# Graph convolution: one product for three turns of the vectors, one for three vector components, operands copied dense by ScalarE

## Chip, core and metric

One NeuronCore of a Trainium2 chip runs the whole program. The metric is the device time of one execution in microseconds, taken as the median of the runs shown. Engines are named as in the profile: PE (TensorE), DVE (VectorE), ACT (ScalarE), POOL (GpSimd), SP (SyncE).

## What is computed

A graph network of four layers on 12,500 nodes and 400,000 edges, each layer added to x and normalised. The change concerns the last layer, an equivariant convolution over edges. A node's 32 features are 8 scalars and 8 vectors of three components. Each edge has a weight (from which a small network makes 384 radial numbers) and a unit direction r. Cut to what matters:

```python
R = relu(abs_distances[:, None] @ w1 + b1) @ w2 + b2      # 384 numbers an edge
Y = spherical_harmonics(rel_vec)                          # of the direction
Fj = features[src]
for i, (mo, lo) in enumerate(RS):                         # out: 8 scalars, 8 vectors
    for j, (mi, li) in enumerate(RS):                     # in: 8 scalars, 8 vectors
        for k, lf in enumerate(range(abs(lo - li), lo + li + 1)):
            acc += _NORM[i] * einsum('euv,ef,evi,ofi->euo', Rb[..., k], Yf, Fb, C)
out = zeros.at[dst].add(msg)
```

The kernel writes this with v·r (how far a vector points along the direction), v x r (the crossed vector), v itself and the scalars: 256 radial numbers weigh 16 factors (8 scalars, 8 times v·r) and 128 weigh, for each component, 16 numbers (8 of v, 8 of v x r).

## The kernel before

Edges come sorted by destination in groups of 512: 128 partitions by `PER` = 4 columns j. The convolution (`convolve`) works through 832 groups, in 208 turns of a loop that has `SLOTS` = 4 groups written out; `s` is the group's place in the turn, `c = s % 2` chooses one of two buffers. `turns` writes the first and the last turn apart.

`after_hops` normalises x and makes the table of rows to be gathered: `CONV` = 88 floats a node, 8 scalars and then five blocks of 16 floats (`BLOCK`), of which the first 8 hold vector component 0, 1, 2, 0, 1 and the other 8 are zero. It is stored to `conv_dram`.

In `convolve` each engine has its own program and they meet in semaphores.

- SP loads a group's edges (`rows`, 8 floats each: source, place, weight, direction, and the first direction components again) when `rows_free` is 2 (one from ACT, one from DVE) and then its weights.
- POOL gathers the 512 source rows (`far`) by four indirect DMAs when `far_free` is 2. Between the second and the third it does `fold_products` for a group two back: it waits for `products_made` and adds the halves of `products_a`.
- ACT makes `hidden` for the group after (L2098), copies the scalars of `far` into `factors` (L2114), makes `minus_local` (L2117), `away` (L2127) and `hot` (L2135), the matrix that sends edges to nodes.
- PE makes the radial numbers of the next group (L2156, L2157) when `radial_free` allows and `hidden` is ready, and then sums the messages of the group before into `part` (L2168).
- DVE does the rest, in `one_group`. For group s: three products of vectors with shifted directions, `turned` (L2220, 96 elements each). For the group before, p: `finish_b` (L2206, sums `products_b` over 16, 1536 elements read) and `finish_a` (L2198, 512 read, waits for the fold). For s: `factors` (L2258, v·r) and the cross product (L2261), written into the zeros of `far`. For p: `along_r` (L2227). For s: `products_a` (L2270, 1024). For p: `add_own` (L2232), which lets PE sum. For s: three products, `product_b` (L2275, 512 each, one per component), between them two calls of `accumulate` (L2239, 32 elements each) which add the node sums of group s - 2 to `sums`.

`step` gives each DVE instruction a count on one semaphore and `wait(n)` waits for that count. The queue is in order: whatever stands behind a wait is issued after it. The end of the group is this:

```python
product_b(2).then_inc(radial_free[c], 1)
if added:
    wait(n_added)
    dve.sem_inc(part_free[c], 1)
```

At the end of a turn there follow `wait()`, the loop's branch and `steps.restart()`, which clears the count.

Of the kernel before, what the change touches and what calls it, by code (L numbers as in the profile page):

```python
# [24 lines left out]
P = 128  # L25
# [38 lines left out]
CONV = MUL + 5 * BLOCK  # L64
# [1850 lines left out]
def after_hops(nc, k):  # L1915
# [67 lines left out]
def convolve(nc, k):  # L1983

    with stage(nc, k) as ctx:
# [20 lines left out]
        sum_b = sb("sum_b", [P, 3, PER, MUL], 2)  # L2006
# [8 lines left out]
        factors_ready, factors_free = sem("factors_ready", 2), sem("factors_free", 2)  # L2015
# [66 lines left out]
        def _(act):  # L2082
            for c in range(2):
# [4 lines left out]
                act.sem_inc(factors_free[c], 1)  # L2088
# [16 lines left out]
            def one_turn(i, first, last):  # L2105
                for s in range(SLOTS):
# [6 lines left out]
                    act.wait_ge(factors_free[c], turn(i, s, 2))  # L2113
                    act.copy(factors[c][:, :, 0:MUL], far[s][:, :, 0:MUL]).then_inc(copied, 1)  # L2114
# [8 lines left out]
                    act.wait_ge(copied, 1 + HALVES)  # L2123
# [10 lines left out]
                    act.wait_ge(copied, 1 + HALVES + PER)  # L2134
# [50 lines left out]
        def _(dve):  # L2185
# [16 lines left out]
            def finish_b(i, s):  # L2202

                dve.wait_ge(radial_free[s % 2], turn(i, s, 2) + 1)
                dve.sem_inc(far_free[s % SLOTS], 1)
                return step(dve.tensor_reduce(sum_b[s % 2][:].rearrange("p o j u -> p (o j u)"),  # L2206
                                              products_b[:].rearrange("p o j u m -> p (o j u) m"),
                                              AX.X, ALU.add))

            def direction(s, at):  # L2210

                return spread(rows[s % SLOTS][:, :, 3 + at:6 + at], 3, MUL)

            def blocks(s, at):

                return far[s][:, :, MUL + at * BLOCK:MUL + (at + 3) * BLOCK].rearrange("p j (o m) -> p j o m", m=BLOCK)

            def turn_vectors(s, n, at_v, at_r):

# [219 lines left out]
```

## Time and profile before

| | us |
|---|---|
| median of three runs | 29652.48 |
| lowest, highest | 29636.92, 29660.63 |
| the profiled execution | 29833.74 |
| its span, first to last instruction | 29831.7 |

The profiled execution is 0.6% above the median. The page gives busy time by engine, then the span in 40 slices; the convolution is the last seven or eight of them, where DVE stands at 9 tenths. A group of instructions is shown by line, engine, operation, the names written and read, how many there were, busy time, mean duration and the idle time before them. The timeline gives a start and a duration for each. Instructions of one engine are pipelined, so that a start can lie before the end of the one in front; instructions that only handle semaphores, registers and branches are not shown and appear as idle time if nothing runs beneath them. A matmul's end is modelled.

### The profile page before, as it was taken

The page shows a single profiled execution, that of the slowest core. Times are in us where ns is not written, and L with a number is a line of the kernel's source. Part 1 is how long each engine was busy: PE and PEld are TensorE (multiplying, and loading weights), DVE is VectorE, ACT ScalarE, POOL GpSimd, SP SyncE. Part 2 cuts the span into 40 slices and gives each one's busy share as a digit, 9 for nine tenths or more (in the row PEclk, how much of TensorE's full clock was granted, in tenths as well). Part 3 has the DMA queues.
Part 4 walks back from the last instruction along what each step waited for, and adds up shares of the span by engine and source line. Part 5 has one row for each costly group of instructions (what it writes and reads, how often), then busy time and mean ns, then how long its engine had stood idle before and what let it go on. Part 6 is the DMA issues. An engine that isn't in the chain of part 4 may idle for free. (4 is left out here: it accounts for less than half of the span.)

```text
span 29831.7 us, 294521 instructions
## 1 busy us (share of the span) xinstructions
PE 13941.6 (47%) x65171; PEld 13225.7 (44%) x65172; DVE 11715.7 (39%) x26884; ACT 5681.8 (19%) x18021; POOL 17107.9 (57%) x17490
## 2 busy tenths in 40 slices
PE   1333333333333357777433333333333358888887
PEld 1233323333333357777433333333333347777777
DVE  1376511111111145555211111111111159999999
ACT  6411222100000011111000000000000025555554
POOL 2677766366666620000366666666666667777777
PEclk8555555555555577777555555555555568888888
DMA  1111111322222210000000000200000032222223
GB/s 44 15 15 14 15 14 15 24 58 58 59 58 59 59 32 20 19 20 20 13 11 12 11 12 11 11 13 11 11 12 11 11 33 50 50 50 50 50 50 47
DMA packets 1840283, 855.51 MB, mean 29 GB/s; under 512 B 1295920, under 2 KB 1624849, under 8 KB 1839380
## 3 DMA queue, kind: packets, MB, share of 16 engines
q0 software_dynamic: 532480, 382.75, 9.8%
q1 hardware_dynamic: 1307008, 471.30, 7.1%
q14 instruction: 86, 0.70, 0.0%
q10 hardware_dynamic: 692, 0.49, 0.0%
q8 instruction: 17, 0.28, 0.0%
HBM read 757.65 MB, written 96.92 MB: 29 GB/s over the span
## 5 line engine op out<-in xcount | busy, mean ns | idle before, releaser
L937 POOL DMA_INDIRECT hop_far<-hop_rows,hop_index x6656 | 6280.0, 944 | 7187.6 <-issue 6005.5
L973 PE MATMUL hop_total<-hop_far,hop_hot 128*128 128x32 f32 x13312 | 3127.2, 376 | 6433.4 <-issue 3640.6
L973 PEld LDWEIGHTS hop_total<-hop_far,hop_hot 128*128 128x128 f32 x13312 | 3080.7, 322 | 6481.2 <-issue 6479.8
L743 POOL DMA_INDIRECT weighted_far<-in_x_dram,weighted_rows x3328 | 3410.8, 1025 | 2052.5 <-issue 1475.5
L952 DVE TENSOR_TENSOR hop_hot<-hop_iota,local_of_edge 128x512 f32<-128x512 f32 x1664 | 1092.8, 688 | 8405.0 <-DMA rows_by_src<-push_row,push_index 7087.8
L1048 POOL DMA_INDIRECT rows_by_src<-push_row,push_index x3328 | 3186.4, 957 | 1741.3 <-issue 1520.7
L2048 POOL DMA_INDIRECT conv_far<-conv_rows x3328 | 3174.6, 954 | 1050.5 <-issue 810.1
L2156 PE MATMUL conv_radial_a<-radial,conv_hidden 128*128 128x256 f32 x6656 | 2893.2, 523 | 792.3 <-DVE conv_products_b L2275 562.9
L1097 PE MATMUL push_near<-far_rows_sb,push_turned 128*128 x6656 | 1689.4, 436 | 3218.2 <-DVE push_turned L1075 1750.3
L826 PE MATMUL weighted_total<-weighted_message,weighted_hot 128*128 128x33 f32 x6656 | 1569.7, 399 | 3450.7 <-issue 1621.5
L1097 PEld LDWEIGHTS push_near<-far_rows_sb,push_turned 128*128 128x128 f32 x6656 | 1601.5, 327 | 3306.1 <-issue 3304.6
L826 PEld LDWEIGHTS weighted_total<-weighted_message,weighted_hot 128*128 128x128 f32 x6656 | 1486.5, 327 | 3534.7 <-issue 3534.3
L2156 PEld LDWEIGHTS conv_radial_a<-radial,conv_hidden 128*128 128x128 f32 x6656 | 1856.6, 327 | 858.4 <-issue 856.8
L2157 PEld LDWEIGHTS conv_radial_b<-radial,conv_hidden 128*128 128x128 f32 x6656 | 1992.7, 332 | 171.6
L924 ACT COPY hop_index<-source_of_edge 128x4 int32 (+1 forms) x1664 | 291.8, 193 | 9310.2 <-DMA rows_by_src<-push_row,push_index 7431.5
L2157 PE MATMUL conv_radial_b<-radial,conv_hidden 128*128 128x128 f32 x6656 | 1855.3, 367 | 0.0
L2275 DVE TENSOR_TENSOR conv_products_b<-conv_radial_b,conv_far 128x512 f32<-128x512 f32 x2496 | 1694.7, 679 | 0.0
L1071 DVE TENSOR_TENSOR push_place<-push_place,push_trash 128x4 f32<-128x4 f32 x832 | 137.7, 166 | 3939.5 <-DMA push_place<-place_by_dst 3437.7
L2206 DVE TENSOR_REDUCE conv_sum_b<-conv_products_b 128x96 f32<-128x1536 f32 x832 | 1449.3, 1742 | 0.2 <-DVE conv_products_b L2275 0.2
L849 ACT ACTIVATE weighted_message<-weighted_far,weighted_rows 128x32 f32<-128x32 f32 x3328 | 828.6, 311 | 2513.0 <-DMA weighted_far<-in_x_dram,weighted_rows 1819.1
L2068 POOL TENSOR_TENSOR conv_folded_a<-conv_products_a 128x512 f32<-128x512 f32 x832 | 1053.8, 1267 | 350.3 <-issue 232.8
L1770 PE MATMUL att_part<-att_b_message,att_b_hot 128*128 128x132 f32 x7040 | 1247.3, 335 | 4.3 <-DVE att_b_message L1675 4.3
(250 smaller groups left out, 20408.4 us busy)
## 6 DMA issues: line engine op xcount, KB each, us to landing
push_line<-local_by_group SPq DMA_DIRECT2D x832, 256.0 KB
hop_far<-hop_rows,hop_index POOLq DMA_INDIRECT x6656
conv_weights<-weight_by_group SPq DMA_DIRECT2D x832, 128.0 KB
att_far<-rows_by_src SPq DMA_DIRECT2D x880, 80.0 KB
weighted_far<-in_x_dram,weighted_rows POOLq DMA_INDIRECT x3328
rows_by_src<-push_row,push_index POOLq DMA_INDIRECT x3328
conv_far<-conv_rows POOLq DMA_INDIRECT x3328
weighted_rows<-edges_by_dst SPq DMA_DIRECT2D x1664, 8.0 KB
```

The costliest lines, as they stand in the source:

```text
L743: pool.indirect_dma_start(far[s][:, j, :], None, table, bass.IndirectOffsetOnAxis(ap=rows[s][:, j, 0:1].bitcast(I32), axis=0)).then_inc(ga ...
L826: last = pe.matmul(total[:].rearrange("p n c -> p (n c)")[:, bass.ds(at[s * HALVES + j // COLUMNS], width)], hot[s][:, j, :], message[s][: ...
L937: pool.indirect_dma_start(far[s][:, j, :], None, table, bass.IndirectOffsetOnAxis(ap=index[s][:, j:j + 1], axis=0)).then_inc(gathered[s], 16)
L973: last = pe.matmul(total[:].rearrange("p n c -> p (n c)")[:, bass.ds(at[s * HALVES + j // COLUMNS] * F, F)], hot[s][:, j, :], far[s][:, j, ...
L1048: pool.indirect_dma_start(k.rows_by_src, bass.IndirectOffsetOnAxis(ap=index[s][:, j:j + 1], axis=0), row[s][:, j, :], None).then_inc(writt ...
L1097: last = pe.matmul(near[:, b, j * FAR:(j + 1) * FAR], turned[b][:, :, j], k.far_rows[:].rearrange("p b w -> p (b w)")[:, bass.ds(at[s * HA ...
L1770: last = pe.matmul(part[s % 2][:, 0:HEADS * W], b_hot[b][:, j, :], b_message[b][:, j, :], start=(j == 0), stop=(j == PER - 1))
L2048: pool.indirect_dma_start(far[s][:, j, :], None, k.conv_dram, bass.IndirectOffsetOnAxis(ap=rows[s][:, j, 0:1].bitcast(I32), axis=0)).then_ ...
L2156: pe.matmul(radial_a[:, c, j, :], hidden[c][:, :, j], k.radial[:, 0:256], start=True, stop=True)
L2157: last = pe.matmul(radial_b[:, c, j, :], hidden[c][:, :, j], k.radial[:, 256:384], start=True, stop=True)
L2206: return step(dve.tensor_reduce(sum_b[s % 2][:].rearrange("p o j u -> p (o j u)"), products_b[:].rearrange("p o j u m -> p (o j u) m"), AX ...
L2275: return dve.tensor_tensor(products_b[:, o], radial_b[:, c].rearrange("p j (u m) -> p j u m", m=BLOCK), spread(blocks(s, 0)[:, :, o, :], 2 ...
```

## The change

The gathered row becomes 64 floats: 8 scalars and seven components of 8 floats (0, 1, 2, 0, 1, 2, 0), without zeros. ACT copies, for each group, the three shifted directions of an edge into `around` (3 x 3), the vector components into the first halves of `pair` (3 components of 16) and, as before, the scalars into `factors`; it then releases a new semaphore `taken`. `rows_free` comes from ACT alone now, and `far_free` from DVE comes right behind `turned`. A semaphore `used` tells ACT that `around`, `pair` and `factors` of a slot may be written again. On DVE one product of 288 elements makes all of `turned`, one of 1536 makes all of `products_b`, whose order is by column and then component. The second `accumulate` stands behind it.

```diff
-CONV = MUL + 5 * BLOCK
+CONV = MUL + 7 * MUL
...
+def windows(tile, first, dims):
+
+    whole = tile[:]
+    return bass.AP(whole.tensor, whole.offset + first, [list(whole.ap[0])] + [list(d) for d in dims])
...
-            s.step(dve.memset(table[:], 0.0))
-            s.wait()
             s.step(dve.tensor_copy(table[:, :, 0:MUL], k.x[:, :, 0:MUL]))
-            for o in range(5):
-                at = MUL + o * BLOCK
+            for o in range(7):
+                at = MUL + o * MUL
                 s.step(dve.tensor_copy(table[:, :, at:at + MUL], vectors[:, :, o % 3, :]))
...
-        turned = [sb(f"turned_{n}", [P, PER, 3, MUL], 2) for n in range(3)]
-        factors = sb("factors", [P, PER, 2 * MUL], 2)
+        turned = sb("turned", [P, PER, 3, 3, MUL], 2)
+        factors = sb("factors", [P, PER, 2 * MUL], SLOTS)
+        pair = sb("pair", [P, PER, 3, BLOCK], SLOTS)
+        around = sb("around", [P, PER, 3, 3], SLOTS)
...
-        products_b = sb("products_b", [P, 3, PER, MUL, BLOCK], 1)[0]
+        products_b = sb("products_b", [P, PER, 3, MUL, BLOCK], 1)[0]
...
-                sp.sem_inc(rows_free[s], 2)
+                sp.sem_inc(rows_free[s], 1)
...
-                    sp.wait_ge(rows_free[s], 2)
+                    sp.wait_ge(rows_free[s], 1)
...
-                    act.wait_ge(factors_free[c], turn(i, s, 2))
-                    act.copy(factors[c][:, :, 0:MUL], far[s][:, :, 0:MUL]).then_inc(copied, 1)
+                    if not first:
+                        act.wait_ge(used[s], i)
+                    act.copy(around[s][:], windows(rows[s], 3, [(BY_DST, PER), (1, 3), (1, 3)])).then_inc(copied, 1)
+                    act.copy(pair[s][:, :, :, 0:MUL], far[s][:, :, MUL:4 * MUL].rearrange("p j (o m) -> p j o m", m=MUL)
+                             ).then_inc(copied, 1)
+                    act.copy(factors[s][:, :, 0:MUL], far[s][:, :, 0:MUL]).then_inc(copied, 1)
...
-                    act.wait_ge(copied, 1)
-                    act.sem_inc(factors_ready[c], 1)
+                    act.wait_ge(copied, 3)
+                    act.sem_inc(taken[s], 1)
                     act.sem_inc(far_free[s], 1)
...
-                dve.sem_inc(far_free[s % SLOTS], 1)
...
+            def turn_vectors(s):
+
+                return step(dve.tensor_tensor(
+                    turned[s % 2][:].rearrange("p j n o m -> p (j n o m)"),
+                    windows(far[s], MUL, [(CONV, PER), (2 * MUL, 3), (1, 3 * MUL)]),
+                    windows(around[s], 0, [(1, PER * 9), (0, MUL)]), ALU.mult))
...
-                n_along = turn_vectors(s, 0, 0, 0)
-                turn_vectors(s, 1, 2, 1)
-                n_turned = turn_vectors(s, 2, 1, 2)
+                dve.wait_ge(taken[s], i + 1)
+                n_turned = turn_vectors(s)
...
                 wait(n_turned)
-                n_crossed = step(dve.tensor_tensor(blocks(s, 0)[:, :, :, MUL:BLOCK], turned[1][c][:], turned[2][c][:],
+                dve.sem_inc(far_free[s], 1)
+                n_factors = step(dve.tensor_reduce(factors[s][:, :, MUL:2 * MUL],
+                                                   turned[c][:, :, 0].rearrange("p j o v -> p j v o"), AX.X, ALU.add))
+                n_crossed = step(dve.tensor_tensor(pair[s][:, :, :, MUL:BLOCK], turned[c][:, :, 1], turned[c][:, :, 2],
                                                    ALU.subtract))
...
-                    dve.sem_inc(rows_free[p % SLOTS], 1)
+                    dve.sem_inc(used[p % SLOTS], 1)
                     add_own(p)
-                wait(n_crossed)
-                step(product_b(0))
+                if added:
+                    n_added = accumulate(i, s - 2, 0, bins[0])
                 wait(n_products)
                 dve.sem_inc(products_made, 1)
-                dve.sem_inc(factors_free[c], 1)
+                wait(n_crossed)
+                dve.tensor_tensor(products_b[:].rearrange("p j o u m -> p (j o u m)"),
+                                  spread(radial_b[:, c], 2, 3),
+                                  spread(pair[s][:].rearrange("p j o m -> p (j o) m"), 2, MUL), ALU.mult
+                                  ).then_inc(radial_free[c], 1)
                 if added:
-                    n_added = accumulate(i, s - 2, 0, bins[0])
-                step(product_b(1))
-                if added:
-                    for h in range(1, HALVES):
-
-                        wait(n_added)
-                        n_added = accumulate(i, s - 2, h, bins[h])
-                product_b(2).then_inc(radial_free[c], 1)
-                if added:
+                    wait(n_added)
+                    n_added = accumulate(i, s - 2, 1, bins[1])
                     wait(n_added)
                     dve.sem_inc(part_free[c], 1)
```

## Rows read from the trace of the kernel before

**Rows 1.** The page: busy time of each engine over the whole span, times, share, instructions

```profile
PE 13941.6 (47%) x65171; PEld 13225.7 (44%) x65172; DVE 11715.7 (39%) x26884; ACT 5681.8 (19%) x18021; POOL 17107.9 (57%) x17490
```

**Rows 2.** Windows: busy us of each engine in this stretch of the convolution

```profile
25000.00:29500.00 4500.00, 3697.93 (x16369) 3445.37 (x16368) 4487.77 (x10231) 2329.57 (x6139) 3465.88 (x3411) 0.86 0.24 50
```

**Rows 3.** Timeline, DVE, one group: start, us, engine, line, op, out<-in, count

```profile
26902.76 0.58 DVE L2220 TENSOR_TENSOR conv_turned<-conv_far,conv_rows 128x96 f32<-128x96 f32 x3
26903.27 1.74 DVE L2206 TENSOR_REDUCE conv_sum_b<-conv_products_b 128x96 f32<-128x1536 f32 x1
26904.93 0.67 DVE L2198 TENSOR_REDUCE conv_message<-conv_folded_a 128x64 f32<-128x512 f32 x1
26905.52 0.25 DVE L2258 TENSOR_REDUCE conv_factors<-conv_turned 128x32 f32<-128x96 f32 x1
...
26905.86 0.25 DVE L2227 TENSOR_TENSOR conv_message<-conv_rows,conv_message 128x96 f32<-128x96 f32 x1
26906.03 1.21 DVE L2270 TENSOR_TENSOR conv_products_a<-conv_radial_a,conv_factors 128x1024 f32<-128x1024 f32 x1
26907.16 0.24 DVE L2232 TENSOR_TENSOR conv_message<-conv_message,conv_sum_b 128x96 f32<-128x96 f32 x1
26907.33 0.68 DVE L2275 TENSOR_TENSOR conv_products_b<-conv_radial_b,conv_far 128x512 f32<-128x512 f32 x1
26907.93 0.17 DVE L2239 TENSOR_TENSOR sums<-sums,conv_part 128x32 f32 x1
26908.02 0.68 DVE L2275 TENSOR_TENSOR conv_products_b<-conv_radial_b,conv_far 128x512 f32<-128x512 f32 x1
...
26908.72 0.68 DVE L2275 TENSOR_TENSOR conv_products_b<-conv_radial_b,conv_far 128x512 f32<-128x512 f32 x1
26909.32 0.58 DVE L2220 TENSOR_TENSOR conv_turned<-conv_far,conv_rows 128x96 f32<-128x96 f32 x3
```

**Rows 4.** Timeline, DVE: the last group of a turn, its start and its end

```profile
26915.88 0.58 DVE L2220 TENSOR_TENSOR conv_turned<-conv_far,conv_rows 128x96 f32<-128x96 f32 x3
...
26921.74 0.17 DVE L2239 TENSOR_TENSOR sums<-sums,conv_part 128x32 f32 x1
26921.83 0.68 DVE L2275 TENSOR_TENSOR conv_products_b<-conv_radial_b,conv_far 128x512 f32<-128x512 f32 x1
26922.58 0.60 DVE L2220 TENSOR_TENSOR conv_turned<-conv_far,conv_rows 128x96 f32<-128x96 f32 x3
```

**Rows 5.** The page, costliest groups: line, op, names, count, busy, mean ns, idle

```profile
L2206 DVE TENSOR_REDUCE conv_sum_b<-conv_products_b 128x96 f32<-128x1536 f32 x832 | 1449.3, 1742 | 0.2 <-DVE conv_products_b L2275 0.2
```

**Rows 6.** Timeline, DVE, after the last turn, where each step is waited for

```profile
29790.22 0.68 DVE L2198 TENSOR_REDUCE conv_message<-conv_folded_a 128x64 f32<-128x512 f32 x1
29790.93 0.26 DVE L2227 TENSOR_TENSOR conv_message<-conv_rows,conv_message 128x96 f32<-128x96 f32 x1
...
29791.92 0.53 DVE L2239 TENSOR_TENSOR sums<-sums,conv_part 128x32 f32 x2 [0.44 <-issue]
```

**Rows 7.** Timeline, ScalarE (ACT): first copy of the group that DVE takes up at 26922.58

```profile
26919.30 0.22 ACT L2114 COPY conv_factors<-conv_far 128x32 f32<-128x32 f32 x1
```

**Rows 8.** Timeline, GpSimd (POOL): fold running behind (first two) and in the middle

```profile
29745.00 1.27 POOL L2068 TENSOR_TENSOR conv_folded_a<-conv_products_a 128x512 f32<-128x512 f32 x1
...
29751.18 1.26 POOL L2068 TENSOR_TENSOR conv_folded_a<-conv_products_a 128x512 f32<-128x512 f32 x1
...
26907.47 1.26 POOL L2068 TENSOR_TENSOR conv_folded_a<-conv_products_a 128x512 f32<-128x512 f32 x1 [0.43 <-issue]
```

**Rows 9.** Timeline, DVE, near the stage's end: a group that starts on a late landing

```profile
29752.99 0.60 DVE L2220 TENSOR_TENSOR conv_turned<-conv_far,conv_rows 128x96 f32<-128x96 f32 x3 [0.19 <-DMA conv_far<-conv_rows]
```

**Rows 10.** Timeline between the hops and the convolution: table of rows and its store

```profile
24231.13 7.25 DVE L1931 MEMSET rows_of_conv<- 128x8624 f32 x1 [1.86 <-issue]
...
24238.89 3.00 DVE L1936 COPY rows_of_conv<-x 128x784 f32<-128x784 f32 x5
...
24242.39 16.45 SPq L1251 DMA_DIRECT2D conv_rows<-rows_of_conv  x1
```

More of the change, by code:

```diff
@@ L2014, in convolve @@
         radial_ready, radial_free = sem("radial_ready", 2), sem("radial_free", 2)
-        factors_ready, factors_free = sem("factors_ready", 2), sem("factors_free", 2)
+        taken, used = sem("taken", SLOTS), sem("used", SLOTS)
         hot_ready = sem("hot_ready", 2)
@@ L2204, in finish_b, with direction @@
                 dve.wait_ge(radial_free[s % 2], turn(i, s, 2) + 1)
-                dve.sem_inc(far_free[s % SLOTS], 1)
-                return step(dve.tensor_reduce(sum_b[s % 2][:].rearrange("p o j u -> p (o j u)"),
-                                              products_b[:].rearrange("p o j u m -> p (o j u) m"),
+                return step(dve.tensor_reduce(sum_b[s % 2][:].rearrange("p j o u -> p (j o u)"),
+                                              products_b[:].rearrange("p j o u m -> p (j o u) m"),
                                               AX.X, ALU.add))
[L2210 to L2218, printed above, removed]
-                return step(dve.tensor_tensor(turned[n][s % 2][:], blocks(s, at_v)[:, :, :, 0:MUL],
-                                              direction(s, at_r), ALU.mult))
+            def direction(s):
+                return spread(around[s % SLOTS][:, :, 0, :], 3, MUL)
+            def turn_vectors(s):
[3 more added lines that the diff above has]
+                    windows(around[s], 0, [(1, PER * 9), (0, MUL)]), ALU.mult))
             def vector_out(s):
@@ L2226, in along_r @@
             def along_r(s):
-                return step(dve.tensor_tensor(vector_out(s), direction(s, 0),
+                return step(dve.tensor_tensor(vector_out(s), direction(s),
                                               spread(message[s % 2][:, :, 4, :], 2, 3), ALU.mult))
             def add_own(s):
-                dve.tensor_tensor(vector_out(s), vector_out(s), sum_b[s % 2][:].rearrange("p o j u -> p j o u"),
+                dve.tensor_tensor(vector_out(s), vector_out(s), sum_b[s % 2][:],
                                   ALU.add).then_inc(message_ready[s % 2], 1)
@@ L2256, in one_group @@
                     n_a = finish_a(i, p)
-                wait(n_along)
-                n_factors = step(dve.tensor_reduce(factors[c][:, :, MUL:2 * MUL],
-                                                   turned[0][c][:].rearrange("p j o v -> p j v o"), AX.X, ALU.add))
                 wait(n_turned)
-                n_crossed = step(dve.tensor_tensor(blocks(s, 0)[:, :, :, MUL:BLOCK], turned[1][c][:], turned[2][c][:],
+                dve.sem_inc(far_free[s], 1)
+                n_factors = step(dve.tensor_reduce(factors[s][:, :, MUL:2 * MUL],
+                                                   turned[c][:, :, 0].rearrange("p j o v -> p j v o"), AX.X, ALU.add))
+                n_crossed = step(dve.tensor_tensor(pair[s][:, :, :, MUL:BLOCK], turned[c][:, :, 1], turned[c][:, :, 2],
                                                    ALU.subtract))
@@ L2265, in one_group @@
                     n_out = along_r(p)
-                dve.wait_ge(factors_ready[c], turn(i, s, 2))
                 dve.wait_ge(radial_ready[c], turn(i, s, 2))
@@ L2271, in one_group @@
                     products_a[:], radial_a[:, c].rearrange("p j (q m) -> p j q m", m=2 * MUL),
-                    spread(factors[c][:], 2, 2 * MUL), ALU.mult))
-                def product_b(o):
-                    return dve.tensor_tensor(
-                        products_b[:, o], radial_b[:, c].rearrange("p j (u m) -> p j u m", m=BLOCK),
-                        spread(blocks(s, 0)[:, :, o, :], 2, MUL), ALU.mult)
+                    spread(factors[s][:], 2, 2 * MUL), ALU.mult))
                 if before:
                     wait(max(n_out, n_sum))
-                    dve.sem_inc(rows_free[p % SLOTS], 1)
+                    dve.sem_inc(used[p % SLOTS], 1)
                     add_own(p)
-                wait(n_crossed)
-                step(product_b(0))
+                if added:
+                    n_added = accumulate(i, s - 2, 0, bins[0])
                 wait(n_products)
                 dve.sem_inc(products_made, 1)
-                dve.sem_inc(factors_free[c], 1)
-                if added:
-                    n_added = accumulate(i, s - 2, 0, bins[0])
-                step(product_b(1))
-                if added:
-                    for h in range(1, HALVES):
-                        wait(n_added)
-                        n_added = accumulate(i, s - 2, h, bins[h])
-                product_b(2).then_inc(radial_free[c], 1)
-                if added:
+                wait(n_crossed)
[3 more added lines that the diff above has]
+                                  ).then_inc(radial_free[c], 1)
+                if added:
+                    wait(n_added)
+                    n_added = accumulate(i, s - 2, 1, bins[1])
                     wait(n_added)
```

7 lines of the change are left out of this document (3 added, 4 removed).

## The prediction

> **What bounds the kernel now.** The profile's first two parts say that no engine is busy for the whole span [rows 1], so the question is the stage. The change touches only `after_hops` and `convolve`, and the convolution fills the last fifth of the span. The table of windows for 4500 us of it shows VectorE (DVE) busy 4487.77 us, 99.7%; TensorE is at 82% and GpSimd at 77% [rows 2]. So this stage's time is DVE's instruction stream, and what is to be counted is its time from one start to the next, not durations, since neighbours overlap.
>
> The DVE timeline of one group of 512 edges gives these steps [rows 3], from each start to the following one: three `turned` products 0.51 us together; `sum_b` 1.66; `finish_a` 0.59; `factors`, `crossed` (left out there, 26905.69) and `along_r` 0.17 each; `products_a` 1.13; `add_own` 0.17; `product_b(0)` 0.60; `accumulate` 0.09; `product_b(1)` 0.60; `accumulate` 0.10; `product_b(2)` 0.60. Sum 6.56 us (26902.76 to 26909.32). The group whose end is also the end of a loop turn takes 6.70 (26915.88 to 26922.58) [rows 4]. The page's `sum_b` row counts 832 groups [rows 5], so 208 turns of four: 3 x 6.56 + 6.70 = 26.38 us a turn.
>
> What a size costs: the steps of 0.095 (32 elements), 0.17 (96), 0.60 (512), 1.13 (1024) and 1.66 us (1536) lie on one line, 0.065 us plus 1.04 ns an element [rows 3]. Strided operands (`turned`, `along_r`), broadcast ones, PSUM ones and dense ones are all on it.
>
> **The change part by part.**
>
> *One `turned` product for three.* 288 elements once: 0.065 + 288 x 1.04 ns = 0.365 us for 0.51. Saves 0.145 a group.
>
> *One `products_b` for three.* 1536 elements are 1.66, the step of `sum_b` [rows 3], for 3 x 0.60 = 1.80. Saves 0.14. Its operands stay a broadcast PSUM array and a broadcast SBUF array, both kinds that are on the line already.
>
> *Where the second `accumulate` goes.* This is the part that decides. Before, it is issued under `product_b(2)`, which covers it: it costs 0.10 of the step, and the wait for its end before `part_free` is released is also covered, since `product_b(2)` runs on. After, it is the last instruction of the group, behind the whole `products_b`, and `wait(n_added)` stands between it and the next group's `turned`. Now its whole 0.17 us is on the path, then the sequencer's way out of that wait: release `part_free`, wait for `gathered`, wait for the new `taken`, issue. Nothing covers that. I call this gap G. The trace does not show it in the steady state. From below: `finish_a` ends at 29790.90 and `along_r`, which waits for it alone, starts at 29790.93: 0.03 us. From above: two accumulates in a row, each waited for, with register work and another wait between, take 0.53 for 2 x 0.17: 0.19 between them [rows 6], and 0.06 more if one wait more costs as much again: 0.25. I take 0.16, near the upper row, as it has the same sort of work in it. The group is then 0.365 + 1.66 + 0.59 + 3 x 0.17 + 1.13 + 0.17 + 0.10 + 1.66 + 0.17 + G = 6.36 + G = 6.52 us: of 0.285 saved by merging, only 0.04 is left.
>
> At the end of a turn the gap is longer, as the loop's branch, the clearing of the step counter and its registers come after that wait. That way is seen whole: the second accumulate ends at 26921.74 + 0.17 = 26921.91 and the next `turned` starts at 26922.58, 0.67 us later [rows 4]. Before, `product_b(2)` ran until 26922.51 beneath it and only about 0.15 was lost (6.70 against 6.56). After, all of it is open, with one more wait: 0.67 + 0.06 = 0.73 (up to 0.93, if the new wait's number has to be made in registers too). The group is 6.36 + 0.73 = 7.09 for 6.70.
>
> A turn: 3 x 6.52 + 7.09 = 26.65 for 26.38, +0.27 us, times 208 = **+56 us**. With G = 0.03 and 0.67 it is 3 x 6.39 + 7.03 = 26.20, -37 us; with 0.25 and 0.93, 3 x 6.61 + 7.29 = 27.12, +154 us.
>
> The Trainium skill speaks against both halves of this. Its page VectorE: DVE Perf Modes, section The DRAIN you can't avoid, says that the next operation does not start until the pipe is empty and that a semaphore between two operations costs nothing extra. By that the exposed wait would be free, and the sum would lie at the low end or under it. The same page's errata section gives an fp32 tensor-tensor instruction (N + 151) cycles at 0.96 GHz: 0.157 us fixed; four instructions fewer a group would then be 0.63 us, an estimate from that page, some 520 us in all. The rows show starts only 0.60 apart where a duration is 0.68 [rows 3]; so most of that fixed part is hidden already, and the trace disagrees for a stream that is never drained.
>
> *ScalarE's two more copies and the wait for them.* `pair` has 96 elements, `around` 36. The copy of 32 takes 0.22 us [rows 7]; none of the three is likely to pass 0.4, so `taken` comes at most 1.2 us after the copies begin at 26919.30. DVE takes up that group at 26922.58 [rows 4]: over 2 us are left. Cost 0 in the steady state. ScalarE itself is at 2329.57 of 4500 [rows 2], and adds under 0.7 of 6.56 us. Its wait for `used` asks for a group four back: 0. Behind it on ScalarE are `minus_local`, `away` and `hot`, for which TensorE waits a group later: covered. If the cover were gone, DVE would lose up to 0.7 us a group.
>
> *Gathers and loads.* Rows of 256 bytes for 352, the same four gathers. `far` and `rows` come free earlier (the first after `turned`, the second by ScalarE alone), so SP may load earlier. GpSimd is held by `fold_products`, which waits for `products_a`: not faster. Its own floor is seen where it runs behind, fold to fold 29745.00 to 29751.18 = 6.18 us, with no idle time listed before the fold; normally 0.43 is idle there [rows 8]. 6.18 is below 6.52, so it doesn't bind, and there was no 6.18 to gain either. `products_made` is released at the same place behind `products_a`.
>
> *`accumulate(0)`* goes ahead of `products_b`: its `part_ready` is two groups old. 0. TensorE sees `radial_free` about 0.25 us earlier after `add_own`. 0 for the end.
>
> *Last groups.* At the stage's end about a dozen groups have late gathers: the timeline has DVE waiting for the landing itself, as at 29752.99 [rows 9]. Now ScalarE's copies come in between, some 0.5 us each time: +6 us (0 to +13).
>
> *Between the stages.* The memset of 7.25 us goes, two more of the 0.60 us copies come, and the store, now 73% of the bytes behind a 16.45 us issue, may save 0 to 4.5, taken as 3 [rows 10]. -9 us (-6 to -11).
>
> **The sum.** 56 + 6 - 9 = +53 us. The profiled execution has 29833.74 us (span 29831.7), 0.6% above the median 29652.48; against its own time the forecast is 29887 us. Stage times are bound by fixed instruction times, so the same 53 us goes on the median: 29705 us. The bounds give -37 - 11 = -48 and 154 + 13 - 6 = +161: 29604 to 29813.
>
> **The rivals.**
> 1. *The wait at the group's end is nearly free* (G near 0.03, the loop's overhead not longer than now): 29604 to 29620 us. For it: the 0.03 row [rows 6]. Against: the 0.67 us at the turn is read directly and nothing is left to hide it.
> 2. *Each instruction removed brings more than its share of the pitch.* If the fixed part were all of 0.68 - 512 x 1.04 ns = 0.15 us, four fewer give 0.6 us a group for the 0.285 above, another 0.315 x 832 = 260 us: 29445 us. Against: five sizes on one line. That is the page's rule above, as far as rows can price it.
> 3. *Slower: DVE waits for `taken`.* ScalarE comes to its copies in order, after `hide`, which waits for the weights. Were the gathers' landing or the weights over 2 us later than now, each group would wait for ScalarE; at 0.5 us a group that is 416 us: 30120 us. Against: the 2 us of room.
>
> **How the numbers follow.** Forecast 0.74 (mechanism as told, -48 to +161), rival 1 0.10 (its end of that range or a little under), rival 2 or another gain 0.08, rival 3 0.08. A difference under 0.2%, 59 us, can't be told from none here. The forecast lies almost on that line: of its 0.74 I give 0.38 to slower and 0.36 to same. Same: 0.36 + 0.10 = 0.46; slower: 0.38 + 0.08 = 0.46; faster 0.08. The range 29604 to 29813 holds the forecast and rival 1, some 0.82; I keep 29600 to 29815.
>
> **What would show it.** In the profile after: `turned` at about 0.44 us and `products_b` at about 1.74 a piece, 832 each; in the DVE timeline a gap of 0.1 to 0.25 us before each `turned` and one of 0.7 to 0.9 at each turn, DVE's share in the windows falling to some 95%; a turn of 26.6 to 26.7 us. It is wrong if the gap is under 0.1 or a row leaves the line, if an idle time of DVE is put down to ScalarE, or if fold to fold nears 6.2.

## The result, and the profile after

The changed kernel takes 29737.51 us (median of 12 runs, 29698.96 to 29792.63), the kernel before in the same 12 rounds 29652.66: +85 us between the medians. The ratio is 1.0031, with a 95% interval of 1.0023 to 1.0039. It is slower, by a little more than the 59 us that the prediction took as the least that can be told from nothing. The forecast had been 29705, +53.

The profiled execution of the changed kernel has a span of 29716.6 us. That it is shorter than the span of the profiled execution before (29831.7) lies ahead of the part that was changed: the convolution's first `turned` starts at 24068.47 us there, at 24278.98 before. So the two are compared from that part on.

The page: busy time of each engine, then the two costliest groups of DVE (line, engine, operation, names, count, busy time, mean ns, idle before them).

```profile
PE 14044.8 (47%) x65171; PEld 13287.3 (45%) x65172; DVE 11532.7 (39%) x23557; ACT 5918.2 (20%) x19685; POOL 17144.8 (58%) x17490
...
L2287 DVE TENSOR_TENSOR conv_products_b<-conv_radial_b,conv_pair 128x1536 f32<-128x1536 f32 x832 | 1455.2, 1749 | 0.2 <-issue 0.2
L2214 DVE TENSOR_REDUCE conv_sum_b<-conv_products_b 128x96 f32<-128x1536 f32 x832 | 1452.2, 1745 | 0.2 <-DVE sums L2245 0.2
```

DVE has 3327 instructions fewer than in [rows 1], four a group, and is busy 183 us less. `products_b` is one instruction of 1749 ns beside `sum_b` of 1745 ns (1742 in [rows 5]): 1536 elements take the same time whether they are reduced or multiplied. DVE's work did become less. Now the windows for the same 4500 us as in [rows 2] (PE, PEld, DVE, ACT, POOL, granted clock, DMA share, GB/s):

```profile
25000.00:29500.00 4500.00, 3716.85 (x16055) 3427.27 (x16053) 4264.50 (x7357) 2482.23 (x7355) 3431.45 (x3344) 0.84 0.20 41
```

DVE was busy 4487.77 us of them and is now busy 4264.50, 94.8%. It waits 235 us and still bounds the stage. Where it waits is in its timeline (start, us, engine, line, operation, names, count, idle time before it); first the end of a turn and the group after it:

```profile
26761.56 0.17 DVE L2245 TENSOR_TENSOR sums<-sums,conv_part 128x32 f32 x1
26762.47 0.46 DVE L2224 TENSOR_TENSOR conv_turned<-conv_far,conv_around 128x288 f32<-128x288 f32 x1 [0.74 <-issue]
26762.85 1.75 DVE L2214 TENSOR_REDUCE conv_sum_b<-conv_products_b 128x96 f32<-128x1536 f32 x1
...
26766.74 0.25 DVE L2238 TENSOR_TENSOR conv_message<-conv_message,conv_sum_b 128x96 f32<-128x96 f32 x1
26766.91 0.18 DVE L2245 TENSOR_TENSOR sums<-sums,conv_part 128x32 f32 x1
26767.01 1.75 DVE L2287 TENSOR_TENSOR conv_products_b<-conv_radial_b,conv_pair 128x1536 f32<-128x1536 f32 x1
26768.67 0.17 DVE L2245 TENSOR_TENSOR sums<-sums,conv_part 128x32 f32 x1
26769.07 0.46 DVE L2224 TENSOR_TENSOR conv_turned<-conv_far,conv_around 128x288 f32<-128x288 f32 x1 [0.22 <-DVE sums L2245]
```

And the next end of a turn:

```profile
26782.26 0.46 DVE L2224 TENSOR_TENSOR conv_turned<-conv_far,conv_around 128x288 f32<-128x288 f32 x1 [0.22 <-DVE sums L2245]
...
26789.38 0.46 DVE L2224 TENSOR_TENSOR conv_turned<-conv_far,conv_around 128x288 f32<-128x288 f32 x1 [0.74 <-DVE sums L2245]
```

From one `turned` to the next a group inside a turn takes 6.60 us (26762.47 to 26769.07; 6.56 in [rows 3]) and one at a turn's end 7.12 (26782.26 to 26789.38; 6.70 in [rows 4]). Before `turned` stand idle times: 0.22 us in each group, where [rows 3] has none, and 0.74 at a turn, where [rows 4] has 0.07. Both stand behind the second `accumulate` (26768.67, 26761.56). The listing by lines, for 2000 us of this stage, adds them up:

```profile
L2224 DVE TENSOR_TENSOR conv_turned<-conv_far,conv_around 128x288 f32<-128x288 f32 x298 | 136.7, 459 | 105.3 <-DVE sums L2245 59.1 <-issue 46.3
```

105.3 us idle before 298 `turned`; that is all of DVE's idle time there.

Ahead of the stage, from the last step of the normalisation on (SPq is the store's issue):

```profile
24030.50 3.42 DVE L1221 TENSOR_TENSOR x<-norm_centred,norm_spread 128x3136 f32<-128x3136 f32 x1
...
24034.44 4.22 DVE L1940 COPY rows_of_conv<-x 128x784 f32<-128x784 f32 x7
...
24039.17 10.10 SPq L1257 DMA_DIRECT2D conv_rows<-rows_of_conv  x1
...
24068.47 0.46 DVE L2224 TENSOR_TENSOR conv_turned<-conv_far,conv_around 128x288 f32<-128x288 f32 x1 [10.41 <-ACTq L2130]
```

From that step to the first `turned` it is 37.97 us (24030.50 to 24068.47). Before it was 53.14 (24225.84 to 24278.98): the memset of 7.25 us and 1.86 idle in front of it are gone, the store's issue takes 10.10 for 16.45 us [rows 10], and two more copies have come. From the first `turned` to the update behind the convolution it is 5613.74 us (24068.47 to 29682.21) for 5518.32 (24278.98 to 29797.30): +95.4. With -15.2 that makes +80 of the 85 us; the other 5 are within the interval (68 to 116 us).

### The profile page after: what moved, and what is told of

Read it like the earlier page. It is cut to its first block and busy times, and to the rows that moved or that the text cites. A ratio compares the mean times of both kernels' runs of the same rounds, so it can differ in the third digit from the quotient of the medians.

```text
span 29716.6 us, 293058 instructions
## 1 busy us (share of the span) xinstructions
PE 14044.8 (47%) x65171; PEld 13287.3 (45%) x65172; DVE 11532.7 (39%) x23557; ACT 5918.2 (20%) x19685; POOL 17144.8 (58%) x17490
## 5 line engine op out<-in xcount | busy, mean ns | idle before, releaser
L2165 PE MATMUL conv_radial_a<-radial,conv_hidden 128*128 128x256 f32 x6656 | 2952.7, 533 | 635.1 <-DVE conv_products_b L2287 554.6
L2287 DVE TENSOR_TENSOR conv_products_b<-conv_radial_b,conv_pair 128x1536 f32<-128x1536 f32 x832 | 1455.2, 1749 | 0.2 <-issue 0.2
L2214 DVE TENSOR_REDUCE conv_sum_b<-conv_products_b 128x96 f32<-128x1536 f32 x832 | 1452.2, 1745 | 0.2 <-DVE sums L2245 0.2
```

The source lines that it names most:

```text
L2165: pe.matmul(radial_a[:, c, j, :], hidden[c][:, :, j], k.radial[:, 0:256], start=True, stop=True)
L2214: return step(dve.tensor_reduce(sum_b[s % 2][:].rearrange("p j o u -> p (j o u)"), products_b[:].rearrange("p j o u m -> p (j o u) m"), AX ...
L2287: dve.tensor_tensor(products_b[:].rearrange("p j o u m -> p (j o u m)"), spread(radial_b[:, c], 2, 3), spread(pair[s][:].rearrange("p j o ...
```

## The experiments

The kernels ran on more than one occasion, and the time of the kernel before was not the same in all (29652.66, 27341.17, 29625.73, 27372.80 us), because of stages ahead of the convolution: its first `turned` starts between 24019 and 24279 us in some traces and between 21776 and 21827 in the others. The convolution itself takes the same in both, within 5 us: the version with early accumulates takes 5258.5 us from the first `turned` to the update where its total is 27075.62 us, and 5263.8 (with one wait fewer) where it is 29366.42. Each kernel is therefore compared with the runs of the kernel before that were made beside it, and group lengths come from the traces.

The theory was that the time is lost where the group's last instruction is an `accumulate` that is waited for with nothing running over it; such a wait is called open below, and one under a running instruction covered. The rivals were the merged products themselves, ScalarE's copies with their new wait, and another engine close behind.

### Both accumulates early, in the changed kernel

```diff
                     n_out = along_r(p)
+                if added:
+                    n_added = accumulate(i, s - 2, 0, bins[0])
...
                     add_own(p)
                 if added:
-                    n_added = accumulate(i, s - 2, 0, bins[0])
+                    wait(n_added)
+                    n_added = accumulate(i, s - 2, 1, bins[1])
...
                 if added:
                     wait(n_added)
-                    n_added = accumulate(i, s - 2, 1, bins[1])
-                    wait(n_added)
                     dve.sem_inc(part_free[c], 1)
```

> The changed kernel, with the two accumulates moved ahead: the first behind along_r, the second behind add_own, so that products_b is the last VectorE instruction of a group and runs over everything the sequencer does at the group's and the turn's end. Theory (the changed kernel lost its time at the uncovered end of the group: 0.17 us of the last accumulate and a gap of 0.22, 0.74 at a turn): every group takes 6.60 - 0.17 - 0.22 + 0.10 = 6.30 us, also at a turn, so 208 x (26.91 - 25.20) = 356 us less than the changed kernel, about 29380 us, and faster than the kernel before by some 270. VectorE is then busy over 99% again. Rival A (the merged products or ScalarE's copies are what costs): the time stays within 50 us of the changed kernel. Rival B (another engine is just behind): GpSimd's fold to fold of 6.2 or TensorE's radial numbers take over, and the group stays at 6.4 or more, 29460 us or above.

Measured: 27075.62 us beside 27341.17, 0.990 (0.9885 to 0.9915), -266 us. DVE's timeline of one group:

```profile
24704.21 0.24 DVE L2233 TENSOR_TENSOR conv_message<-conv_around,conv_message 128x96 f32<-128x96 f32 x1
24704.38 0.17 DVE L2245 TENSOR_TENSOR sums<-sums,conv_part 128x32 f32 x1
...
24705.61 0.23 DVE L2238 TENSOR_TENSOR conv_message<-conv_message,conv_sum_b 128x96 f32<-128x96 f32 x1
24705.78 0.17 DVE L2245 TENSOR_TENSOR sums<-sums,conv_part 128x32 f32 x1
24705.88 1.74 DVE L2290 TENSOR_TENSOR conv_products_b<-conv_radial_b,conv_pair 128x1536 f32<-128x1536 f32 x1
24707.54 0.44 DVE L2224 TENSOR_TENSOR conv_turned<-conv_far,conv_around 128x288 f32<-128x288 f32 x1
```

Neither `accumulate` (24704.38, 24705.78) has idle time behind it, and `turned` starts 1.66 us after `products_b` (24705.88 to 24707.54), as [rows 3] have it for 1536 elements. A group takes 6.29 us, and there is no longer a difference at a turn. The windows of 2000 us:

```profile
24500.00:26500.00 2000.00, 1667.37 (x7632) 1567.68 (x7632) 2000.00 (x3500) 1181.23 (x3499) 1609.49 (x1591) 0.91 0.22 44
```

DVE is busy 2000.00 of 2000.00. The same merged products and the same copies are in this kernel, so they are not what costs (rival A). Rival B asked for 6.4 us or more. GpSimd is nearer than before, though not the bound; two folds of its timeline:

```profile
24712.21 1.27 POOL L2074 TENSOR_TENSOR conv_folded_a<-conv_products_a 128x512 f32<-128x512 f32 x1 [0.19 <-DVEq L2288]
...
24718.49 1.26 POOL L2074 TENSOR_TENSOR conv_folded_a<-conv_products_a 128x512 f32<-128x512 f32 x1 [0.17 <-DVEq L2288]
```

They are 6.28 us apart, at DVE's pace, and still 0.17 of it is idle before the fold.

### The same order of the last two instructions in the kernel before

```diff
                 step(product_b(1))
+                product_b(2).then_inc(radial_free[c], 1)
                 if added:
                     for h in range(1, HALVES):
 
                         wait(n_added)
                         n_added = accumulate(i, s - 2, h, bins[h])
-                product_b(2).then_inc(radial_free[c], 1)
                 if added:
                     wait(n_added)
```

> The kernel before with one edit: the second accumulate stands behind product_b(2) instead of in front of it; three turned products, three product_b and the wide rows stay. Theory: the same loss appears without the rest of the change. A group takes 6.56 - 0.10 + 0.17 + a gap of 0.15 (one wait fewer in it than in the changed kernel, no taken) = 6.78, and at a turn 6.63 + 0.67 = 7.30, so 3 x 6.78 + 7.30 = 27.64 us a turn for 26.39, +260 us: 29915 us. Rival A (the order of the last two instructions does not matter): within 30 us of the kernel before.

Measured: 27600.09 beside 27341.17 us, 1.0092 (1.0077 to 1.0107), +259 us. The first group here ends a turn:

```profile
25004.32 0.59 DVE L2220 TENSOR_TENSOR conv_turned<-conv_far,conv_rows 128x96 f32<-128x96 f32 x3
...
25010.79 0.17 DVE L2239 TENSOR_TENSOR sums<-sums,conv_part 128x32 f32 x1
25011.63 0.60 DVE L2220 TENSOR_TENSOR conv_turned<-conv_far,conv_rows 128x96 f32<-128x96 f32 x3 [0.68 <-DVE sums L2239]
...
25018.10 0.18 DVE L2239 TENSOR_TENSOR sums<-sums,conv_part 128x32 f32 x1
25018.43 0.60 DVE L2220 TENSOR_TENSOR conv_turned<-conv_far,conv_rows 128x96 f32<-128x96 f32 x3 [0.15 <-DVE sums L2239]
```

In this kernel with nothing else of the change the gap is there: 0.15 us behind the `accumulate` at 25018.10 and 0.68 behind that at 25010.79, which ends a turn. The latter group takes 7.31 us (25004.32 to 25011.63), the one after it 6.80. One pair of lines put the other way round costs 0.9% of the whole program. This shows the mechanism by itself. That expected and measured differ by 1 us is luck: the interval is some 40 us to either side, and the groups by themselves are 271 us longer (medians over the stage: 6.79 and 7.32 us, for 6.56 and 6.70), of which the last groups gave some back.

### One wait fewer in the gap

```diff
-                dve.wait_ge(gathered[s], (i + 1) * (16 * PER))
-
                 dve.wait_ge(taken[s], i + 1)
```

> The changed kernel without VectorE's own wait for gathered: taken is released by ScalarE only after its own wait for gathered, so the order is kept with one wait fewer in the gap before turned. Theory: what counts in the gap is how many things the sequencer handles one after another, so the gap falls from 0.22 to 0.15 and from 0.74 to 0.67, 832 x 0.07 = 58 us less than the changed kernel, about 29680 us. Rival: the gap is one fixed latency of draining the engine and the time stays, 29738 us.

Measured: 27368.31 beside 27341.17 us, 1.0011 (1.0002 to 1.0020), +27 us, where the changed kernel has +85: 58 less, as expected, though the interval leaves some 25 us to either side of the 27 alone. The traces are sharper: from the first `turned` to the update it is 5547.2 us for 5613.7.

```profile
25004.69 0.17 DVE L2245 TENSOR_TENSOR sums<-sums,conv_part 128x32 f32 x1
25005.51 0.46 DVE L2224 TENSOR_TENSOR conv_turned<-conv_far,conv_around 128x288 f32<-128x288 f32 x1 [0.65 <-DVE sums L2245]
...
25011.72 0.17 DVE L2245 TENSOR_TENSOR sums<-sums,conv_part 128x32 f32 x1
25012.04 0.46 DVE L2224 TENSOR_TENSOR conv_turned<-conv_far,conv_around 128x288 f32<-128x288 f32 x1
...
25018.56 0.46 DVE L2224 TENSOR_TENSOR conv_turned<-conv_far,conv_around 128x288 f32<-128x288 f32 x1
```

The gap is 0.15 us (25011.72 + 0.17 to 25012.04) for 0.22, and 0.65 for 0.74 at a turn; a group takes 6.52. So the gap is no fixed latency: one more satisfied wait in it costs 0.07 us, and 0.09 at a turn. The same edit was made where nothing is open:

> The version with both accumulates early, and without VectorE's own wait for gathered. In the changed kernel that wait cost 0.07 us a group; here it is handled under the running products_b. Theory: it costs nothing where it is covered, so a group stays at 6.29 us and the time within 10 us of the version with both accumulates early, 0.99 of the kernel before. Rival (a wait costs its 0.07 us wherever it stands): 6.22 us a group, 58 us less, 0.988.

Measured: 29366.42 beside 29625.73 us, 0.9912 (0.9896 to 0.9929). Its group is 6.29 us as without the edit. The rival's 0.988 lies outside the interval, and its group would be 6.22 us: a wait that is handled under a running instruction costs nothing here.

### Three products for one, accumulates between them

```diff
+                def product_b(o):
+                    return dve.tensor_tensor(
+                        products_b[:, :, o], radial_b[:, c].rearrange("p j (u m) -> p j u m", m=BLOCK),
+                        spread(pair[s][:, :, o, :], 2, MUL), ALU.mult)
...
```

with `product_b(0)`, `accumulate(0)`, `product_b(1)`, `accumulate(1)`, `product_b(2)` in the kernel before's order.

> The changed kernel with products_b as three products of 512 again (into the new layout, from pair) and the accumulates between them as before; ScalarE's copies, the single turned product and the narrow rows stay. Theory: a group is the one before less what the single turned product saves, 6.56 - 0.14 = 6.42, at a turn 6.42 + 0.2 = 6.62, so 25.88 us a turn for 26.39, 106 us less, and some 25 less outside the groups: 29520 us, 220 below the changed kernel although it has two instructions more a group. Rival A (ScalarE's copies or the wait for taken cost the time): it stays near 29740.

Measured: 27218.22 beside 27341.17 us, 0.9954 (0.9939 to 0.9970), -123 us, so some 208 below the changed kernel.

```profile
25000.55 0.44 DVE L2224 TENSOR_TENSOR conv_turned<-conv_far,conv_around 128x288 f32<-128x288 f32 x1
...
25006.36 0.67 DVE L2284 TENSOR_TENSOR conv_products_b<-conv_radial_b,conv_pair 128x512 f32<-128x512 f32 x1
25006.96 0.44 DVE L2224 TENSOR_TENSOR conv_turned<-conv_far,conv_around 128x288 f32<-128x288 f32 x1
...
25013.60 0.46 DVE L2224 TENSOR_TENSOR conv_turned<-conv_far,conv_around 128x288 f32<-128x288 f32 x1
```

A group takes 6.41 us and at a turn 6.64 (25006.96 to 25013.60). The version with two instructions more a group is faster, because the last of them covers the end. ScalarE's copies and `taken` are in it, and the group is as short as it was expected to be without a cost for them.

### Both accumulates behind

```diff
-                if added:
-                    n_added = accumulate(i, s - 2, 0, bins[0])
                 wait(n_products)
...
                 if added:
+                    n_added = accumulate(i, s - 2, 0, bins[0])
                     wait(n_added)
                     n_added = accumulate(i, s - 2, 1, bins[1])
```

> The changed kernel with the first accumulate moved behind products_b too, so that two waited steps stand open at the group's end. Theory: the first one loses its 0.10 of covered step and costs 0.17 plus a gap of 0.15 with register work in it, as in the tail of the kernel before: 6.60 + 0.23 = 6.82 us, 7.35 at a turn, 188 us above the changed kernel, 1.0095 of the kernel before. Rival (draining the engine once a group is the price, however many steps stand there): only the 0.07 of difference between covered and open length, 60 us above the changed kernel.

Measured: 29981.99 beside 29625.73 us, 1.0122 (1.0105 to 1.0139), +356. The changed kernel ran in the same rounds:

> The changed kernel itself, as the measure for the three beside it: 0.31% above the kernel before, some 85 us.

It took 29701.67, 1.0035 (1.0021 to 1.0049), +76. So the second open step costs 280 us and not 188, half as much again as expected; the groups account for some 258 of it (0.31 us in each).

```profile
25012.72 0.24 DVE L2238 TENSOR_TENSOR conv_message<-conv_message,conv_sum_b 128x96 f32<-128x96 f32 x1
25012.96 1.76 DVE L2285 TENSOR_TENSOR conv_products_b<-conv_radial_b,conv_pair 128x1536 f32<-128x1536 f32 x1
25014.63 0.50 DVE L2245 TENSOR_TENSOR sums<-sums,conv_part 128x32 f32 x2
25015.36 0.46 DVE L2224 TENSOR_TENSOR conv_turned<-conv_far,conv_around 128x288 f32<-128x288 f32 x1 [0.22 <-DVE sums L2245]
...
25022.26 0.46 DVE L2224 TENSOR_TENSOR conv_turned<-conv_far,conv_around 128x288 f32<-128x288 f32 x1 [0.22 <-DVE sums L2245]
```

A group takes 6.90 us (25015.36 to 25022.26), not 6.82. The two accumulates take 0.50 for 2 x 0.17, a gap of 0.16 as expected. The rest is at a place that had not been looked at: `products_b` starts 0.24 us after `add_own` (25012.72 to 25012.96), where 96 elements cost 0.17. `products_made` is released behind the end of `products_a`, and `products_b` is issued after that; in the changed kernel the first `accumulate` ran over just this wait (26766.74, 26766.91, 26767.01), unseen. That this 0.07 us is the uncovered issue is read from the trace; no run takes it away by itself. The rival, that draining the engine once is the whole price, is out: it asked for 60 us.

### How much room ScalarE has

```diff
+                    for n in range(8):
+                        act.copy(spare[:, n], far[s][:, :, MUL:4 * MUL]).then_inc(copied, 1)
                     act.copy(factors[s][:, :, 0:MUL], far[s][:, :, 0:MUL]).then_inc(copied, 1)
```

> The changed kernel with eight more copies of 96 elements on ScalarE in front of taken, written to a spare tile that nothing reads: about 8 x 0.17 = 1.4 us later for taken. Theory: in the changed kernel VectorE starts a group 3.65 us (median) after ScalarE's first copy of it, and the three copies and the release need 0.67, so 3 us are spare: a group stays at 6.60 and 7.12, and only the last twenty or so groups, whose gathers are late, lose about 1 us each: 0 to 20 us above the changed kernel. Rival (ScalarE's release is what VectorE waits for at the group's start): 1.4 x 832 = 1165 us more.

Measured: 29720.52 beside 29625.73 us, 1.0029 (1.0018 to 1.0041); the changed kernel had 1.0035 in the same rounds, its median 19 us lower. In the changed kernel ScalarE's first and last copy of a group are these, 0.51 us from the first start to the last end:

```profile
26765.13 0.22 ACT L2120 COPY conv_around<-conv_rows 128x36 f32<-128x36 f32 x1 [1.65 <-DMA conv_far<-conv_rows]
...
26765.43 0.21 ACT L2123 COPY conv_factors<-conv_far 128x32 f32<-128x32 f32 x1
```

With eight more in front of `taken`:

```profile
25000.21 0.22 ACT L2121 COPY conv_around<-conv_rows 128x36 f32<-128x36 f32 x1 [0.23 <-DMA conv_far<-conv_rows]
...
25000.51 1.47 ACT L2125 COPY conv_spare<-conv_far 128x96 f32<-128x96 f32 x8
25001.89 0.21 ACT L2126 COPY conv_factors<-conv_far 128x32 f32<-128x32 f32 x1
```

`turned` of that group comes at 25004.17, 3.96 us after the first copy, with the old 0.74 of a turn before it, and 0.22 in the group after:

```profile
25004.17 0.46 DVE L2227 TENSOR_TENSOR conv_turned<-conv_far,conv_around 128x288 f32<-128x288 f32 x1 [0.74 <-DVE sums L2248]
...
25010.77 0.46 DVE L2227 TENSOR_TENSOR conv_turned<-conv_far,conv_around 128x288 f32<-128x288 f32 x1 [0.22 <-DVE sums L2248]
```

1.4 us more on ScalarE's way to `taken` cost nothing that can be told from the scatter of the runs; from the first `turned` to the update it is 5617.5 us for 5614.0. The third rival of the prediction is out for this kernel.

### The order alone, in the kernel before

```diff
                     n_out = along_r(p)
+                if added:
+                    n_added = accumulate(i, s - 2, 0, bins[0])
...
                     add_own(p)
+                if added:
+                    wait(n_added)
+                    n_added = accumulate(i, s - 2, 1, bins[1])
                 wait(n_crossed)
                 step(product_b(0))
...
                 step(product_b(1))
                 product_b(2).then_inc(radial_free[c], 1)
```

> The kernel before with both accumulates early (behind along_r and behind add_own), three turned products and three product_b as they were. It tells what the order alone is worth. Theory: inside a turn both accumulates were covered already, so those groups stay at 6.56 us; at a turn the last wait is now served before the three products, which run over the branch, so 6.72 becomes 6.56: 0.16 x 208 = 33 us less, 0.9989 of the kernel before. Then the rest of what the version with early accumulates gained (0.27 us in every group, 222 us) is the merging, and the change's own idea is worth something once nothing stands behind it. Rival (the order is worth most of it): 6.3 to 6.4 us a group, over 130 us less.

Measured: 27354.38 beside 27372.80 us, 0.9995 (0.9986 to 1.0004), -18 us, which can't be told from no change. First the end of a turn, then the end of a group inside one:

```profile
25003.92 1.88 DVE L2277 TENSOR_TENSOR conv_products_b<-conv_radial_b,conv_far 128x512 f32<-128x512 f32 x3
25005.76 0.60 DVE L2220 TENSOR_TENSOR conv_turned<-conv_far,conv_rows 128x96 f32<-128x96 f32 x3
...
25010.53 1.88 DVE L2277 TENSOR_TENSOR conv_products_b<-conv_radial_b,conv_far 128x512 f32<-128x512 f32 x3
25012.32 0.59 DVE L2220 TENSOR_TENSOR conv_turned<-conv_far,conv_rows 128x96 f32<-128x96 f32 x3
```

From the first `product_b` to the next `turned` it is 1.84 us at a turn and 1.79 inside one, and a group inside a turn takes 6.56 (25005.76 to 25012.32). So a group at a turn's end is at 6.61, for 6.70 in [rows 4]: 0.09 of the expected 0.16 came, 19 us in 208 turns. The version with the early accumulates ran beside it:

> The version with both accumulates early once more, beside the one before it, on the same chip: 6.29 us a group, 0.99 of the kernel before, some 270 us less.

27100.26 us, 0.990 (0.9885 to 0.9916), -273. So the order alone is worth about 20 of these, the merging, the narrower rows and the dropped memset about 250 (27354.38 less 27100.26, measured side by side). Of these the groups give 222: 6.56 to 6.29 us in each of 832. The change's own idea is good for 0.9%. The place of the second `accumulate`, 32 elements, turned it into a loss of 0.3%; the first was moved too, but it costs the same 0.10 us step in either place.

## Why the prediction was right

The forecast was +53 us and its range 29600 to 29815; measured was +85, 29737.51. The mechanism was told as it came out. That the total is only 32 us off is in part luck, as errors went against each other. The steps in turn:

- **DVE's stream is the stage's time.** Right: in every kernel here the group's length is DVE's, with DVE 93.0% (both accumulates behind) to 100% busy, and the rest of its time is the gap it makes for itself.
- **Prices from one line of starts.** Right: `turned` came to 0.38 us (26762.47 to 26762.85) for 0.365, `products_b` to 1.66 for 1.66. Durations were told as about 0.44 and 1.74; the page has 459 ns (in the listing) and 1749.
- **The open end.** The mechanism is shown by five runs: both accumulates early, the order in the kernel before, one wait fewer, three products, both behind. Its size was the term that was off: G was put at 0.16 and is 0.22. The extra wait for `taken` was counted as 0.06 for the turn and for the upper bound only. One wait of this kind, that for `gathered`, costs 0.07 in every group (the run with one wait fewer); the middle value left it out. The group became 6.60 for 6.52.
- **At a turn.** 0.74 for 0.73, a group of 7.12 for 7.09. What was read directly from a row came out to 0.01.
- **The turn as a whole**: 3 x 6.60 + 7.12 = 26.92 for 26.38, +0.54, times 208 = +112 us where +56 stood. That is double, and it is still within the bounds of -37 to +154. The sign given for the profile, a turn of 26.6 to 26.7 us, did not come.
- **Between the stages**: -15 for -9 (bounds -6 to -11, so outside): the 1.86 us idle in front of the memset [rows 10] went with it, and the store gained more than its bytes' share.
- **The last groups**: +6 was forecast with 0 as the best, and this was wrong in sign and in its reading. The stage as a whole gained 95 and not 112 us. Beyond the usual length of their place in the turn, the last 25 groups lost 15.4 us in the kernel before and 4.7 in the changed one, 11 of the 17 us; some 2 came at the start and the rest is rounding. Waits for a landing, as in [rows 9], were only 2.4 us of the 15.4. For 12.7 a product of `turned` was running and took up to 2.04 us for the usual 0.25 (the last section). In the changed kernel no `turned` is stretched; its late groups wait for their operands. 2.5 us of that, in two groups, are put down to ScalarE, which the prediction had named as a sign of being wrong; it is too little to matter. The narrower rows are not needed for the gain: with the wide rows and groups of 6.79 us (the order in the kernel before) the last groups lose 2.5 us, and with the narrow rows and groups of 6.29 us some 15.
- The term of the turn was missed by +56, the other two together by -29, and so they covered for each other in part. That the total came nearer than its largest part is the luck named above.

Of the rivals, the free wait is out (0.22 and not 0.03; no turn without its 0.74), and so are the instruction price (the steps of 0.38 and 1.66 us lie on the line) and the wait for ScalarE (eight copies, no cost). The page VectorE: DVE Perf Modes of the Trainium skill says, in the section The DRAIN you can't avoid, that a semaphore between two operations costs nothing extra. This agrees with the covered waits here (0.00 us for the wait taken away where `products_b` runs), and not with the open ones (0.07 us for that same wait, 0.22 for the whole gap). The measurement decides.

## What to carry to other kernels

On an engine that is busy all the time, look at what its sequencer must do after each wait for the engine's own last result, and keep a long instruction queued over it; put short waited steps, and the releases that hang on them, in front of the long one. When instructions are merged, ask what ran under the parts: three pieces with work between them give cover that one piece in front of that work does not. Count time from start to start, and add for an open wait what the sequencer handles in it, priced from a row with the same sort of work.

## What the runs showed of the hardware that was not expected

TensorE's busy share is no measure of its room here. In 2000 us of the stage it was busy 1667 us (83.4%) with groups of 6.29 us, and its share was 82.6% (3716.85 of 4500) with groups of 6.60 and 82.2% in [rows 2] with 6.56. Its work a group is the same, and its mean granted clock was 0.91, 0.84 and 0.86 of full speed. The profile records only full speed (2.4 GHz) and half of it (1.2 GHz) in this stage, so 0.91 is full speed for 82% of the time and 0.84 for 68%: with shorter groups it was granted full speed for more of the time. Why is not shown. A reader who takes the share for fixed work would scale the 82.2% of [rows 2], 5.42 us of a mean group of 6.60, to 86% at 6.29; it was 83.4%.

A product of `turned` that met GpSimd's fold was held until the fold was over. In the kernel before:

```profile
29745.74 1.00 DVE L2220 TENSOR_TENSOR conv_turned<-conv_far,conv_rows 128x96 f32<-128x96 f32 x3
```

The three products take 1.00 us for the usual 0.58. The first of them alone takes 0.67 and ends at 29746.40, 0.13 us after the fold that started at 29745.00 [rows 8]. In this trace 14 products of `turned` take over 0.12 us longer than usual, two at the stage's start and twelve in its last 25 groups, and each of them ends 0.12 or 0.13 us after a fold; in the kernel before with the other order of its last two instructions there are 5, in the one with early accumulates 13, all with the same 0.12 or 0.13. Some of them had begun up to 0.65 us before the fold's recorded start (29701.29, fold 29701.94), and why they are held even so is not shown; starts on GpSimd are rough in this profile. Both `turned` and the fold have their two inputs in SBUF. The `product_b` over which the fold runs in the middle of the stage, with one operand in PSUM, keeps its 0.68 us [rows 3, 8]. This is read from the traces; no run was made for it. It costs 15 us in the kernel before and nothing in the changed one, where no `turned` meets a fold, so an engine off the critical path matters here by when it runs.
